# Softmax attention: ScalarE sums every fourth key tile's exponentials, three waves of ones per head instead of six

## The chip, the cores and the metric

One of the eight cores of a Trainium2 chip runs the whole program. Time is the device time of one execution in microseconds (us). The engines of a core work side by side, each through its own queue in order: TensorE (matrix products, PE in the views, with its weight loads as PEld), VectorE (DVE), ScalarE (ACT), GpSimd (POOL) and SyncE (SP, which issues most DMAs). They wait for each other through semaphores. SBUF is the working memory of 128 partitions; PSUM has eight banks of 128 x 512 numbers, into which TensorE writes.

## The reference

Four layers follow each other on `x` of shape (2, 2048, 512): a Mamba layer (L0), softmax attention (L1) and two linear attentions (L2, L3). The change lies in L1 alone:

```python
q = (xn @ q_w + q_b).reshape(Bx, Tx, H, -1)        # 16 heads of 32
k = (xn @ k_w + k_b).reshape(Bx, Tx, H, -1)
att = jnp.einsum('bnhl,bmhl->bnmh', q, k)
att = att + (1.0 - mask) * -1000000.0
att = jax.nn.softmax(att, axis=2)                  # over the keys
v = ((xn @ v_w + v_b) * src_mask[:, :, None]).reshape(Bx, Tx, H, -1)
y = jnp.einsum('bnmh,bmhl->bnhl', att, v)
```

With 2 batches and 16 heads there are 32 softmax problems of 2048 x 2048, called heads below. The softmax is the exact one: each query's maximum is taken off before the exponential.

## The kernel before, in words

`stage_attention` (from L1123) works through the 32 heads. It computes each head's scores twice.

*First pass, queries on partitions.* `max_mm` (L1263) makes one max tile: 128 queries (`qt`) against 512 keys (`kc`), in one of three PSUM banks `ps_max`. `reduce` (L1394) takes the maximum over the 512 keys on VectorE. 64 such tiles give a head's maxima `mx`; one small reduction (L1400) makes `m_all`, `turn_max` transposes it on TensorE, `first_part` (ScalarE, L1354) and `second_part` (VectorE, L1404) split it into two rows, and SyncE copies these into the stack of query rows by two DMAs (L1219). So the second pass gets its scores with the maximum already taken off.

*Second pass, keys on partitions.* `score_mm` (L1286) makes a tile of 128 keys (`kt`) against 512 queries, in one of three banks `ps_s`; `exp` (ScalarE, L1363) writes its exponentials into `prob`, which has four slots of 128 x 2048. `pv_mm` (L1296) multiplies a whole key tile's exponentials by the values into `ps_o`, which holds the sum over all 16 key tiles.

*Denominators.* GpSimd adds key tiles' exponentials element by element (L1251, in halves of 1024 columns) in groups of 2 or 3 tiles (`SIZES`, L1133), six groups a head. For each group `den_mm` (L1308) multiplies the sum by a matrix of ones and accumulates in `ps_d`: a wave of ones, four matmuls side by side in four column quarters of the array. `copy_o` and `copy_den` (ScalarE, L1369 and L1373) bring the output and the denominators to SBUF, `turn_o` transposes both, `read_o` (VectorE) takes the reciprocal (L1414) and writes the product to `v` (L1419).

*Order.* It is written out by hand. The main loop of TensorE goes over heads `hd` and units `u` (0 to 15), one key tile each. In unit `u` it issues, in turn, four score matmuls of key tile `u + 1` and four max matmuls that belong to the next head (from unit 13, `TURN_MAX`, to the one after that), then `pv_mm` of key tile `u`, and then what falls into this unit: a wave of ones (`DEN_LAG`, 2 units after a group's last key tile), `turn_o` of the head before (`TURN_O`, unit 2) or `turn_max` (unit 13). ScalarE does four exponentials per unit, then `copy_den` (unit 1), `first_part` (unit 13), and `copy_o` after unit 15. VectorE does four reductions per unit. A score matmul waits for the exponential three before it, a max matmul for the reader of the tile three before it (`free_bank`, L1258). Ahead of the first head, 64 max tiles of head 0 and 12 of head 1 are made with nothing else between them.

Of the kernel before, what the change touches and what calls it, by code (L numbers as in the profile page):

```python
# [1122 lines left out]
def stage_attention(nc, a, keep, parts, mask_parts, v):  # L1123

    with ExitStack() as ctx:
# [4 lines left out]
        NMAX = QT * QB  # L1130
        PER = NMAX // QT
        LEAD = 3
        SIZES = (2, 3, 3, 2, 3, 3)  # L1133
        GROUPS = [tuple(range(sum(SIZES[:g]), sum(SIZES[:g + 1]))) for g in range(len(SIZES))]
        NGRP = len(GROUPS)
        GROUP_END = {units[-1]: g for g, units in enumerate(GROUPS)}
        ADDS = sum(2 * (len(units) - 1) for units in GROUPS)
        used, sums = {}, {}
        for g, units in enumerate(GROUPS):
            for n, unit in enumerate(units[1:]):  # L1140
                for half in range(2):
# [4 lines left out]
        SLOTS = 4  # L1146
        HEADS = NB * H1
        TURN_MAX = QT - LEAD
        TURN_O = 2
        DEN_LAG = 2  # L1150
        q_st = [r.sb(f"q_stack{i}", [ROWS, S], F32R) for i in range(3)]
        k_st = [r.sb(f"k_stack{i}", [ROWS, S], F32R) for i in range(3)]
        prob = [r.sb(f"prob{i}", [P, S]) for i in range(SLOTS)]
# [12 lines left out]
        ps_o = r.ps("ps_o", [P, CH])  # L1166
        ps_d = r.ps("ps_d", [P, CH])
        names = ("ones_set rows_set max_in bank_filled bank_read m_done m_first m_second s_mm exp_done "
                 "o_mm o_copied sum_done den_mm den_copied den_turned den_inv den_read v_copied")
# [10 lines left out]
        def bank_items(hd):  # L1180
# [52 lines left out]
        @block.gpsimd  # L1233
        def _(pool):
            def take_v(hd):
                nc.gpsimd.tensor_copy(v_h[hd % 3][:, :, :], v[:, :, hd * DH1:(hd + 1) * DH1]).then_inc(s["v_copied"], 1)

            nc.gpsimd.memset(ones[:, :], 1.0).then_inc(s["ones_set"], 1)
            take_v(0)
            for hd in range(HEADS):  # L1240
                for g, units in enumerate(GROUPS):
                    if hd * NGRP + g >= 2:
                        pool.wait_ge(s["den_mm"], hd * NGRP + g - 1)
                    for n, unit in enumerate(units[1:]):
                        for half in range(2):
                            at = slice(half * HALF, (half + 1) * HALF)
                            pool.wait_ge(s["exp_done"], (hd * QT + unit) * QB + 2 * half + 2)
                            if n:
                                pool.wait_ge(s["sum_done"], hd * ADDS + used[units[n], half])
                            first = pair_sum[g % 2] if n else prob[units[0] % SLOTS]  # L1250
                            nc.gpsimd.tensor_tensor(pair_sum[g % 2][:, at], first[:, at], prob[unit % SLOTS][:, at],  # L1251
                                                    ALU.add).then_inc(s["sum_done"], 1)
                    if g == NGRP // 2 and hd + 1 < HEADS:
                        take_v(hd + 1)

        @block.tensor
        def _(pe):
            def free_bank(seq):  # L1258
                if seq >= BANKS:
                    pe.wait_ge(s["bank_read"], seq - BANKS + 1)  # L1260
                return ps_max[seq % BANKS]

            def max_mm(seq, hd, i):  # L1263
                slot = hd % 3
                if i == 0:
                    pe.wait_ge(stack_in[slot], (hd // 3 + 1) * NSTACK * 16)
                qt, kc = divmod(i, QB)
                nc.tensor.matmul(free_bank(seq)[:, :], q_st[slot][0:ROWS_MAX, qt * P:(qt + 1) * P],  # L1268
                                 k_st[slot][0:ROWS_MAX, kc * CH:(kc + 1) * CH], start=True, stop=True).then_inc(s["bank_filled"], 1)
# [38 lines left out]
            def den_mm(hd, g):  # L1308

                if g == 0 and hd:  # L1310
                    pe.wait_ge(s["den_read"], hd)
                pe.wait_ge(s["sum_done"], hd * ADDS + sums[g])
                for c in range(QB):
                    mm = nc.tensor.matmul(ps_d[c * DH1:(c + 1) * DH1, :], ones[:, :],
                                          pair_sum[g % 2][:, c * CH:(c + 1) * CH], start=(g == 0), stop=(g == NGRP - 1))
                mm.then_inc(s["den_mm"], 1)

            for i in range(NMAX):
# [29 lines left out]
        @block.scalar  # L1348
        def _(act):
            def first_part(seq, hd):  # L1350
                act.wait_ge(s["bank_filled"], seq + 1)
                if hd:
                    act.wait_ge(s["max_in"], hd * 32)
                nc.scalar.activation(m_parts[:, 0, :], ps_max[seq % BANKS][0:QT, 0:P], ACT.Copy, scale=-1.0).then_inc(s["m_first"], 1)  # L1354

            def exp(hd, kt, c):
                n = (hd * QT + kt) * QB + c
                act.wait_ge(s["s_mm"], n + 1)
                if hd * QT + kt >= SLOTS:
                    act.wait_ge(s["o_mm"], hd * QT + kt - SLOTS + 1)  # L1360
                    before, unit = divmod(hd * QT + kt - SLOTS, QT)
                    act.wait_ge(s["sum_done"], before * ADDS + used[unit, c // 2])
                nc.scalar.activation(prob[kt % SLOTS][:, c * CH:(c + 1) * CH], ps_s[n % BANKS][:, :], ACT.Exp).then_inc(s["exp_done"], 1)  # L1363

            def copy_o(hd):
                act.wait_ge(s["o_mm"], (hd + 1) * QT)
                if hd:
                    act.wait_ge(s["den_turned"], hd)
                nc.scalar.activation(o_raw[:, :], ps_o[:, :], ACT.Copy).then_inc(s["o_copied"], 1)  # L1369

            def copy_den(hd):
                act.wait_ge(s["den_mm"], (hd + 1) * NGRP)
                nc.scalar.activation(d_raw[:, :], ps_d[:, :], ACT.Copy).then_inc(s["den_copied"], 1)  # L1373

            first_part(NMAX, 0)
            for c in range(QB):
                exp(0, 0, c)
            for hd in range(HEADS):
                for u in range(QT):
                    for c in range(QB):  # L1380
                        if u + 1 < QT:
                            exp(hd, u + 1, c)
                        elif hd + 1 < HEADS:
                            exp(hd + 1, 0, c)
                    if u == TURN_O - 1 and hd:
                        copy_den(hd - 1)
                    if u == TURN_MAX and hd + 1 < HEADS:
                        first_part(item_at(hd, "turn_max", u), hd + 1)
                copy_o(hd)
            copy_den(HEADS - 1)  # L1390

        @block.vector
        def _(dve):
            def reduce(seq, hd, i):  # L1394
                qt, kc = divmod(i, QB)
# [579 lines left out]
```

## Time and profile before

| | us |
|---|---|
| median of 3 runs (lowest, highest) | 5740.84 (5740.23, 5743.70) |
| the profiled execution: its own time | 5742.74 |
| its span, first to last instruction | 5741.0 |
| mean granted TensorE clock | 0.973 |
| TensorE matmul busy | 5252.8 (91%) |
| VectorE busy | 4120.5 (72%) |
| GpSimd busy | 3280.1 (57%) |
| ScalarE busy | 2812.1 (49%) |

The rows further down come from one profiled execution. Starts are counted from its first instruction. In a row of the timeline, instructions of one line that follow each other are put together: `x4` with 2.06 us means that four of them lasted from the first start to the last end. In brackets stands how long the engine was idle before, and what ended that. The attention stage lies between about 2520 and 4351 us.

### The profile page before, as it was taken

To read this page: it belongs to the slowest core of one execution; us is meant where nothing else is said; L and a number is where in the kernel's file an instruction comes from. 1 tells how busy PE (TensorE), PEld (TensorE's weight loads), DVE (VectorE), ACT (ScalarE), POOL (GpSimd) and SP (SyncE) were. 2 spreads that over 40 slices of the span, in tenths; PEclk is the share of its full clock that TensorE was granted. 3 is DMA by queue.
4 is the path that set the end of the run, shared out by engine and by line. 5 is a ranking of instruction groups with operands and counts; after the bars stand their busy time and mean duration, and the time that the engine had idled before them with its cause. 6 is when DMAs were issued, how large, how long until landed. Compare 5 with 4: busy or idle time off the path is not lost. (4 is left out here: it accounts for less than half of the span.)

```text
span 5741.0 us, 58781 instructions
## 1 busy us (share of the span) xinstructions
PE 5252.8 (91%) x19584; PEld 2496.9 (43%) x19584; DVE 4120.5 (72%) x5430; ACT 2812.1 (49%) x4847; POOL 3280.1 (57%) x2136
## 2 busy tenths in 40 slices
PE   7888989888898869989999999999997899989998
PEld 2333333333333324445455455454543455454545
DVE  6999999999999972357777777777763455545454
ACT  4757566575757523326666666666662131312212
POOL 3879797887979751118888888888883000000000
PEclk9999999999999999979999999999999999999999
DMA  4021211212122114321111111111102301021101
GB/s 169 22 103 49 99 74 52 78 48 103 37 89 82 44 56 159 118 85 23 35 23 35 35 23 35 23 35 29 29 12 105 114 26 62 25 105 35 61 26 52
DMA packets 117503, 346.28 MB, mean 60 GB/s; under 512 B 13040, under 2 KB 14288, under 8 KB 102800
## 3 DMA queue, kind: packets, MB, share of 16 engines
q1 hardware_dynamic: 99280, 294.47, 15.7%
q0 software_dynamic: 9216, 33.56, 1.5%
q10 hardware_dynamic: 8704, 14.50, 0.7%
q8 instruction: 155, 2.54, 0.2%
q14 instruction: 148, 1.21, 0.1%
HBM read 274.29 MB, written 67.67 MB: 60 GB/s over the span
## 5 line engine op out<-in xcount | busy, mean ns | idle before, releaser
L1397 DVE TENSOR_REDUCE attn_mx<-attn_ps_max 128x1 f32<-128x512 f32 x2048 | 1269.5, 682 | 404.7 <-PE attn_ps_max L1268 400.1
L425 POOL TENSOR_TENSOR mamba_hc<-mamba_h,mamba_bc 128x1024 f32<-128x1024 f32 x512 | 1216.7, 2376 | 351.8 <-DVE mamba_h L658 298.0
L1363 ACT ACTIVATE attn_prob<-attn_ps_s 128x512 f32<-128x512 f32 x2048 | 1061.0, 604 | 589.8 <-PE attn_ps_s L1293 586.9
L805 PE MATMUL mamba_y<-mamba_hc,ident 128*128 128x512 f32 x2048 | 1008.2, 616 | 257.3 <-POOL mamba_hc L425 256.4
L1251 POOL TENSOR_TENSOR attn_pair_sum<-attn_prob 128x1024 f32<-128x1024 f32 x384 | 906.7, 2383 | 312.3 <-ACT attn_prob L1363 312.3
L528 ACT ACTIVATE mamba_da<-mamba_dt,mamba_a_neg 128x512 f32<-128x512 f32 x1024 | 689.5, 689 | 685.2 <-DVE mamba_h L658 682.1
L658 DVE TENSOR_TENSOR_SCAN mamba_h<-mamba_da,mamba_state,mamba_h 128x512 f32<-128x512 f32 x768 | 939.3, 1263 | 1.9 <-ACT mamba_da L528 1.9
L1293 PE MATMUL attn_ps_s<-attn_q_stack,attn_k_stack 100*128 100x512 f32 x2048 | 862.2, 424 | 4.2 <-ACT attn_prob L1363 4.2
L1268 PE MATMUL attn_ps_max<-attn_k_stack,attn_q_stack 98*128 98x512 f32 x2048 | 835.4, 415 | 16.5 <-DMA attn_q_stack<-qk_parts 16.0
L805 PEld LDWEIGHTS mamba_y<-mamba_hc,ident 128*128 128x128 f32 x2048 | 373.0, 193 | 838.4 <-POOL mamba_hc L425 421.3
L648 DVE TENSOR_TENSOR mamba_h<-mamba_du,mamba_bc 128x1024 f32<-128x1024 f32 x512 | 618.6, 1208 | 65.7 <-POOL mamba_state L427 57.5
L1251 POOL TENSOR_TENSOR attn_pair_sum<-attn_pair_sum,attn_prob 128x1024 f32<-128x1024 f32 x256 | 604.8, 2386 | 0.0
L1293 PEld LDWEIGHTS attn_ps_s<-attn_q_stack,attn_k_stack 100*128 100x128 f32 x2048 | 387.3, 190 | 455.5 <-ACT attn_prob L1363 232.2
L1304 PE MATMUL attn_ps_o<-attn_prob,attn_v_h 128*32 128x512 f32 x4096 | 546.4, 605 | 0.0
L1268 PEld LDWEIGHTS attn_ps_max<-attn_k_stack,attn_q_stack 98*128 98x128 f32 x2048 | 396.6, 194 | 133.4 <-DVE attn_mx L1397 40.3
L913 POOL TENSOR_TENSOR lin_norm_rstd<-lin_norm_var_eps,neg_half 128x4 f32<-128x4 f32 x16 | 16.1, 1007 | 606.8 <-DVE lin_norm_var_eps L902 606.8
L658 DVE TENSOR_TENSOR_SCAN mamba_h<-mamba_da,mamba_zeros,mamba_h 128x512 f32<-128x512 f32 x256 | 313.1, 1264 | 0.8 <-ACT mamba_da L528 0.8
L913 POOL TENSOR_TENSOR lin_out_norm_rstd<-lin_out_norm_var_eps,neg_half 128x4 f32<-128x4 f32 x16 | 16.1, 1006 | 515.6 <-DVE lin_out_norm_var_eps L902 515.6
L793 PE MATMUL mamba_work<-mamba_w,mamba_zy 128*128 128x512 f32 x512 | 253.9, 623 | 31.6 <-DVE mamba_x_in L676 31.1
L750 PE MATMUL mamba_work<-mamba_xn_t,mamba_w 128*128 128x512 f32 x512 | 249.4, 615 | 1.1 <-ACT mamba_xn_t L463 0.9
L761 PE MATMUL mamba_work<-mamba_xn_t,mamba_w 128*128 128x512 f32 x512 | 242.3, 595 | 0.0
L1651 PE MATMUL lin_mm_bank<-lin_w_q,lin_norm_xn_t 128*128 128x512 f32 x512 | 226.1, 595 | 8.4 <-DVE lin_q L1815 8.4
(232 smaller groups left out, 6077.6 us busy)
## 6 DMA issues: line engine op xcount, KB each, us to landing
mamba_bc<-bc_dram SPq DMA_DIRECT2D x64, 1024.0 KB, 7.3
mamba_w<-in_in_proj_w_T SPq DMA_DIRECT2D x16, 2048.0 KB, 7.8
qk_parts<-qkv_pair POOLq DMA_DIRECT2D x64, 512.0 KB
attn_k_stack<-qk_parts SPq DMA_DIRECT2D x96, 256.0 KB
attn_q_stack<-qk_parts SPq DMA_DIRECT2D x96, 256.0 KB
mamba_x_in<-in_x SPq DMA_DIRECT2D x16, 1024.0 KB, 5.3
mamba_w<-in_out_proj_w_T SPq DMA_DIRECT2D x8, 2048.0 KB, 8.6
lin_norm_x<-x_after_L SPq DMA_DIRECT2D x16, 1024.0 KB, 5.7
```

What stands on the lines that cost most here:

```text
L425: nc.gpsimd.tensor_tensor(hc[:, gs % HC_SLOTS, :, :], h[:, gs % H_SLOTS, :, :], bc[:, g, G:2 * G, :], ALU.mult).then_inc(s["hc_done"], 1)
L528: nc.scalar.activation(da[n % DA_BANKS][:, :], dt[:, ct % 2, :], ACT.Exp, scale=a_neg[:, ct, g * G + j:g * G + j + 1]).then_inc(s["exp_don ...
L648: nc.vector.tensor_tensor(h[:, gs % H_SLOTS, :, :], du[:, :].unsqueeze(1).to_broadcast([P, G, CH]), bc[:, g, 0:G, :], ALU.mult).then_inc(s ...
L658: nc.vector.tensor_tensor_scan(h[:, gs % H_SLOTS, j, :], da[(gs * G + j) % DA_BANKS][:, :], h[:, gs % H_SLOTS, j, :], first, ALU.mult, ALU ...
L793: mm = nc.tensor.matmul(at("out", it, t)[:, :], zy[:, k, t * P:(t + 1) * P], w_view("out", it)[:, k, :], start=(k == 0), stop=(k == CT - 1))
L805: mm = nc.tensor.matmul(y[ct % 2][:, :], ident[:, :], hc[:, gs % HC_SLOTS, j, :], start=(g == 0 and j == 0), stop=(g == NG - 1 and j == G ...
L1251: nc.gpsimd.tensor_tensor(pair_sum[g % 2][:, at], first[:, at], prob[unit % SLOTS][:, at], ALU.add).then_inc(s["sum_done"], 1)
L1268: nc.tensor.matmul(free_bank(seq)[:, :], q_st[slot][0:ROWS_MAX, qt * P:(qt + 1) * P], k_st[slot][0:ROWS_MAX, kc * CH:(kc + 1) * CH], start ...
L1293: nc.tensor.matmul(ps_s[n % BANKS][:, :], k_st[slot][0:ROWS, kt * P:(kt + 1) * P], q_st[slot][0:ROWS, c * CH:(c + 1) * CH], start=True, st ...
L1304: mm = nc.tensor.matmul(ps_o[c * DH1:(c + 1) * DH1, :], v_h[hd % 3][:, kt, :], prob[kt % SLOTS][:, c * CH:(c + 1) * CH], start=(kt == 0), ...
L1363: nc.scalar.activation(prob[kt % SLOTS][:, c * CH:(c + 1) * CH], ps_s[n % BANKS][:, :], ACT.Exp).then_inc(s["exp_done"], 1)
L1397: nc.vector.tensor_reduce(mx[hd % 3][:, qt, kc:kc + 1], ps_max[seq % BANKS][:, :], AX.X, ALU.max).then_inc(s["bank_read"], 1)
```

## The change

Key tiles 3, 7, 11 and 15 of a head are no longer added by GpSimd. Their part of each query's denominator comes from the first pass. The keys of a max tile are regrouped, so that block 3 of four holds just these four key tiles. For that block's tiles VectorE writes the negated maximum (`own_neg`), and ScalarE then makes one more activation on the same PSUM bank (`sum_own`): the exponential with `own_neg` as bias, whose sum over the row goes to `own_sum`. A max matmul that reuses the bank waits for that too. The sum stands against the block's own maximum, so it is scaled by exp(block maximum - head's maximum): GpSimd makes the difference (`make_gap`), ScalarE its exponential (`exp_gap`, after unit 5), GpSimd the product (`scale_own`), and VectorE adds it to the denominators ahead of the reciprocal. The other 12 key tiles form three groups of four. `TURN_O` goes from 2 to 3 and `DEN_LAG` from 2 to 3; the waves of ones then stand in units 7, 12, and 1 of the next head.

```diff
-        SIZES = (2, 3, 3, 2, 3, 3)
-        GROUPS = [tuple(range(sum(SIZES[:g]), sum(SIZES[:g + 1]))) for g in range(len(SIZES))]
-        NGRP = len(GROUPS)
+        OWN = QB - 1
+        SUMMED = [u for u in range(QT) if u % QB != OWN]
+        NGRP = 3
+        GROUPS = [tuple(SUMMED[g * len(SUMMED) // NGRP:(g + 1) * len(SUMMED) // NGRP]) for g in range(NGRP)]
...
-        TURN_O = 2
-        DEN_LAG = 2
+        TURN_O = 3
+        DEN_LAG = 3
+        GAP_AT = 5
...
+            def make_gap(hd):
+                pool.wait_ge(s["m_done"], hd + 1)
+                nc.gpsimd.tensor_tensor(own_gap[:, :], own_neg[hd % 3][:, :, 0], m_all[:, :], ALU.add).then_inc(s["gap_made"], 1)
+
+            def scale_own(hd):
+                pool.wait_ge(s["gap_exp"], hd + 1)
+                pool.wait_ge(s["own_summed"], (hd + 1) * QT)
+                if hd >= 2:
+                    pool.wait_ge(s["den_whole"], hd - 1)
+                nc.gpsimd.tensor_tensor(own_den[hd % 2][:, :], own_sum[hd % 3][:, :], own_gap[:, :], ALU.mult).then_inc(s["own_scaled"], 1)
...
             def free_bank(seq):
                 if seq >= BANKS:
                     pe.wait_ge(s["bank_read"], seq - BANKS + 1)
+                    if SEQ_OWN[seq - BANKS]:
+                        pe.wait_ge(s["own_summed"], OWN_BY[seq - BANKS + 1])
...
-                nc.tensor.matmul(free_bank(seq)[:, :], q_st[slot][0:ROWS_MAX, qt * P:(qt + 1) * P],
-                                 k_st[slot][0:ROWS_MAX, kc * CH:(kc + 1) * CH], start=True, stop=True).then_inc(s["bank_filled"], 1)
+                nc.tensor.matmul(free_bank(seq)[:, :].rearrange("p (a j) -> p a j", j=P), q_st[slot][0:ROWS_MAX, qt * P:(qt + 1) * P],
+                                 k_st[slot][0:ROWS_MAX, :].rearrange("r (a b j) -> r b a j", b=QB, j=P)[:, kc],
+                                 start=True, stop=True).then_inc(s["bank_filled"], 1)
...
+            def sum_own(seq, hd, i):
+
+                act.wait_ge(s["bank_read"], seq + 1)
+                nc.scalar.activation(own_exp[:, :], ps_max[seq % BANKS][:, :], ACT.Exp, bias=own_neg[hd % 3][:, i // QB, :],
+                                     accum_out=own_sum[hd % 3][:, i // QB:i // QB + 1]).then_inc(s["own_summed"], 1)
...
                             exp(hd + 1, 0, c)
+                    for j, tile in enumerate(max_tiles(hd, u)):
+                        if own_block(tile[1]):
+                            sum_own(item_at(hd, "max", u, j), *tile)
                     if u == TURN_O - 1 and hd:
                         copy_den(hd - 1)
                     if u == TURN_MAX and hd + 1 < HEADS:
                         first_part(item_at(hd, "turn_max", u), hd + 1)
+                    if u == GAP_AT:
+                        exp_gap(hd)
                 copy_o(hd)
...
+                to = own_neg[hd % 3][:, qt, :] if own_block(i) else mx[hd % 3][:, qt, kc:kc + 1]
+                nc.vector.tensor_reduce(to, ps_max[seq % BANKS][:, :], AX.X, ALU.max, negate=own_block(i)).then_inc(s["bank_read"], 1)
                 if i == NMAX - 1:
                     dve.wait_ge(s["bank_read"], seq + 1)
+                    nc.vector.tensor_reduce(mx[hd % 3][:, :, OWN:QB], own_neg[hd % 3][:, :, :], AX.X, ALU.max, negate=True
+                                            ).then_inc(s["m_own"], 1)
+                    dve.wait_ge(s["m_own"], hd + 1)
+                    if hd:
+                        dve.wait_ge(s["gap_made"], hd)
...
-                nc.vector.reciprocal(rden[:, :].rearrange("p (t c) -> p t c", c=QB),
-                                     ps_d[:, :].rearrange("p (t c e) -> p t c e", c=QB, e=DH1)[:, :, :, 0]).then_inc(s["den_inv"], 1)
+                dve.wait_ge(s["own_scaled"], hd + 1)
+                nc.vector.tensor_tensor(rden[:, :].rearrange("p (t c) -> p t c", c=QB),
+                                        ps_d[:, :].rearrange("p (t c e) -> p t c e", c=QB, e=DH1)[:, :, :, 0],
+                                        own_den[hd % 2][:, :].rearrange("p (c t) -> p t c", c=QB), ALU.add).then_inc(s["den_whole"], 1)
+                dve.wait_ge(s["den_whole"], hd + 1)
+                dve.sem_inc(s["den_read"], 1)
+                nc.vector.reciprocal(rden[:, :], rden[:, :]).then_inc(s["den_inv"], 1)
                 dve.wait_ge(s["den_inv"], hd + 1)
-                dve.sem_inc(s["den_read"], 1)
```

## Rows read from the trace of the kernel before

**Rows 1.** The page's costliest groups, GpSimd's first sums: x count, busy us, mean ns, idle before.
```profile
L1251 POOL TENSOR_TENSOR attn_pair_sum<-attn_prob 128x1024 f32<-128x1024 f32 x384 | 906.7, 2383 | 312.3 <-ACT attn_prob L1363 312.3
```

**Rows 2.** Stretches: us, busy us of each engine (instructions), granted clock, DMA share, GB/s.
```profile
2524.00:2580.00 56.00, 53.91 (x99) 26.48 (x100) 48.88 (x82) 4.82 (x10) 4.18 (x2) 0.50 0.24 54
2580.00:4295.00 1715.00, 1713.76 (x9654) 857.48 (x9656) 1262.60 (x2090) 1061.84 (x2071) 1468.71 (x649) 1.00 0.12 28
```

**Rows 3.** Line L1354, once a head from head 1: durations ns, first and last start.
```profile
L1354 ACT ACTIVATE attn_m_parts<-attn_ps_max x31: 266/266/268, 2623.2 to 4289.8; 16x128 fp32r<-16x128 f32 x31
```

**Rows 4.** Timeline of a plain unit: start us, us, engine, line.
```profile
3315.41 0.50 PE L1293 MATMUL attn_ps_s<-attn_q_stack,attn_k_stack 100*128 100x512 f32 x1
3315.95 2.06 ACT L1363 ACTIVATE attn_prob<-attn_ps_s 128x512 f32<-128x512 f32 x4 [1.02 <-PE attn_ps_s L1293]
3316.19 2.48 DVE L1397 TENSOR_REDUCE attn_mx<-attn_ps_max 128x1 f32<-128x512 f32 x4 [0.59 <-PE attn_ps_max L1268]
3316.93 0.40 PE L1293 MATMUL attn_ps_s<-attn_q_stack,attn_k_stack 100*128 100x512 f32 x1
3318.48 0.50 PE L1293 MATMUL attn_ps_s<-attn_q_stack,attn_k_stack 100*128 100x512 f32 x1
```

**Rows 5.** Timeline: first score matmuls of a unit with a wave, and of the next.
```profile
3279.95 0.50 PE L1293 MATMUL attn_ps_s<-attn_q_stack,attn_k_stack 100*128 100x512 f32 x1
3283.87 0.50 PE L1293 MATMUL attn_ps_s<-attn_q_stack,attn_k_stack 100*128 100x512 f32 x1
```

**Rows 6.** Timeline of ScalarE: activations with a bias, and a read of the accumulator.
```profile
68.94 0.69 ACT L513 ACTIVATE mamba_dt<-mamba_y,cols 128x512 f32<-128x512 f32 x1 [0.60 <-PE mamba_y L783]
69.53 0.68 ACT L514 ACTIVATE mamba_soft<-mamba_y,cols 128x512 f32<-128x512 f32 x1
...
4691.70 2.00 ACT L1743 ACTIVATE lin_k_t<-lin_k_t,lin_k_max 128x2048 f32<-128x2048 f32 x1 [14.73 <-DVE lin_k_max L1829]
4693.61 0.19 ACT L1743 ACTIVATION_READ_ACCUMULATOR lin_k_t<-lin_k_t,lin_k_max 128x1 f32 x1
4693.70 1.99 ACT L1743 ACTIVATE lin_k_t<-lin_k_t,lin_k_max 128x2048 f32<-128x2048 f32 x1
```

**Rows 7.** Timeline in the last head, where no max tiles are made.
```profile
4337.95 2.07 ACT L1363 ACTIVATE attn_prob<-attn_ps_s 128x512 f32<-128x512 f32 x4 [0.54 <-PE attn_ps_s L1293]
4338.60 0.19 PEld L1293 LDWEIGHTS attn_ps_s<-attn_q_stack,attn_k_stack 100*128 100x128 f32 x1 [0.66 <-ACT attn_prob L1363]
```

**Rows 8.** Timeline of ScalarE at a head's end.
```profile
3297.24 0.60 ACT L1369 ACTIVATE attn_o_raw<-attn_ps_o 128x512 f32<-128x512 f32 x1 [0.59 <-PE attn_ps_o L1304]
3297.74 1.08 ACT L1363 ACTIVATE attn_prob<-attn_ps_s 128x512 f32<-128x512 f32 x2
```

**Rows 9.** Timeline of VectorE after the output is turned.
```profile
3308.30 0.26 DVE L1414 RECIPROCAL attn_rden<-attn_ps_d 128x16 f32<-128x16 f32 x1 [0.94 <-PE attn_ps_d L1283]
3308.71 0.69 DVE L1419 TENSOR_TENSOR v<-attn_ps_max,attn_rden 128x512 f32<-128x512 f32 x1
```

**Rows 10.** Timeline after the maxima are turned; the rows' DMAs, line L1219.
```profile
3345.87 0.27 ACT L1354 ACTIVATE attn_m_parts<-attn_ps_max 16x128 fp32r<-16x128 f32 x1 [0.77 <-PE attn_ps_max L1273]
3346.17 0.28 DVE L1404 SCALAR_TENSOR_TENSOR attn_m_parts<-attn_ps_max,attn_m_parts 16x128 fp32r<-16x128 f32 x1 [0.42 <-ACT attn_m_parts L1354]
3349.62 0.19 PEld L1293 LDWEIGHTS attn_ps_s<-attn_q_stack,attn_k_stack 100*128 100x128 f32 x1 [0.84 <-DMA attn_q_stack<-attn_m_parts]
...
L1219 SPq DMA_DIRECT2D attn_q_stack<-attn_m_parts x64: 502/584/1126, 2565.4 to 4290.9; - x64
DMA to landing us min/median/max: 1.8/1.8/2.5
```

**Rows 11.** Timeline ahead of the first head.
```profile
2554.37 2.47 DVE L1397 TENSOR_REDUCE attn_mx<-attn_ps_max 128x1 f32<-128x512 f32 x4
2554.51 2.59 PE L1268 MATMUL attn_ps_max<-attn_k_stack,attn_q_stack 98*128 98x512 f32 x4
```

**Rows 12.** Timeline at the stage's end.
```profile
4346.58 0.20 PEld L1314 LDWEIGHTS attn_ps_d<-attn_pair_sum,attn_ones 128*32 128x32 f32 x8 [5.67 <-POOL attn_pair_sum L1251]
```

More of the change, by code:

```diff
@@ L1157, in stage_attention @@
         m_all = r.sb("m_all", [P, QT])
+        own_exp = r.sb("own_exp", [P, CH])
+        own_sum = [r.sb(f"own_sum{i}", [P, QT]) for i in range(3)]
+        own_neg = [r.sb(f"own_neg{i}", [P, QT, 1]) for i in range(3)]
+        own_gap = r.sb("own_gap", [P, QT])
+        own_den = [r.sb(f"own_den{i}", [P, QT]) for i in range(2)]
         m_parts = r.sb("m_parts", [QT, 2, P], F32R)
@@ L1168, in stage_attention @@
         names = ("ones_set rows_set max_in bank_filled bank_read m_done m_first m_second s_mm exp_done "
-                 "o_mm o_copied sum_done den_mm den_copied den_turned den_inv den_read v_copied")
+                 "o_mm o_copied sum_done den_mm den_copied den_turned den_inv den_read v_copied "
+                 "m_own gap_made gap_exp own_summed own_scaled den_whole")
         s = {n: r.sem(n) for n in names.split()}
@@ L1189, in bank_items, with own_block @@
             return items
+        def own_block(i):
+            return i % QB == OWN
         BEFORE = NMAX + 1 + LEAD * PER
@@ L1198, in item_at @@
             return first_item[hd] + bank_items(hd).index((kind, u, j))
+        SEQ_OWN = [own_block(i) for i in range(NMAX)] + [False] + [own_block(i) for i in range(LEAD * PER)]
+        for hd in range(HEADS):
+            SEQ_OWN += [kind == "max" and own_block(max_tiles(hd, u)[j][1]) for kind, u, j in bank_items(hd)]
+        OWN_BY = [0]
+        for own_here in SEQ_OWN:
+            OWN_BY.append(OWN_BY[-1] + own_here)
         @block.sync
@@ L1236, in take_v @@
                 nc.gpsimd.tensor_copy(v_h[hd % 3][:, :, :], v[:, :, hd * DH1:(hd + 1) * DH1]).then_inc(s["v_copied"], 1)
+            def make_gap(hd):
[7 more added lines that the diff above has]
+                nc.gpsimd.tensor_tensor(own_den[hd % 2][:, :], own_sum[hd % 3][:, :], own_gap[:, :], ALU.mult).then_inc(s["own_scaled"], 1)
             nc.gpsimd.memset(ones[:, :], 1.0).then_inc(s["ones_set"], 1)
             take_v(0)
+            make_gap(0)
             for hd in range(HEADS):
@@ L1249, in _ @@
                                 pool.wait_ge(s["sum_done"], hd * ADDS + used[units[n], half])
-                            first = pair_sum[g % 2] if n else prob[units[0] % SLOTS]
-                            nc.gpsimd.tensor_tensor(pair_sum[g % 2][:, at], first[:, at], prob[unit % SLOTS][:, at],
+                            first = pair_sum[(hd * NGRP + g) % 2] if n else prob[units[0] % SLOTS]
+                            nc.gpsimd.tensor_tensor(pair_sum[(hd * NGRP + g) % 2][:, at], first[:, at], prob[unit % SLOTS][:, at],
                                                     ALU.add).then_inc(s["sum_done"], 1)
@@ L1254, in _ @@
                         take_v(hd + 1)
+                    if g == 0:
+                        scale_own(hd)
+                if hd + 1 < HEADS:
+                    make_gap(hd + 1)
         @block.tensor
@@ L1314, in den_mm @@
                     mm = nc.tensor.matmul(ps_d[c * DH1:(c + 1) * DH1, :], ones[:, :],
-                                          pair_sum[g % 2][:, c * CH:(c + 1) * CH], start=(g == 0), stop=(g == NGRP - 1))
+                                          pair_sum[(hd * NGRP + g) % 2][:, c * CH:(c + 1) * CH], start=(g == 0), stop=(g == NGRP - 1))
                 mm.then_inc(s["den_mm"], 1)
@@ L1361, in exp @@
                     before, unit = divmod(hd * QT + kt - SLOTS, QT)
-                    act.wait_ge(s["sum_done"], before * ADDS + used[unit, c // 2])
+                    if (unit, c // 2) in used:
+                        act.wait_ge(s["sum_done"], before * ADDS + used[unit, c // 2])
                 nc.scalar.activation(prob[kt % SLOTS][:, c * CH:(c + 1) * CH], ps_s[n % BANKS][:, :], ACT.Exp).then_inc(s["exp_done"], 1)
@@ L1373, in copy_den, with exp_gap @@
                 nc.scalar.activation(d_raw[:, :], ps_d[:, :], ACT.Copy).then_inc(s["den_copied"], 1)
+            def sum_own(seq, hd, i):
+                act.wait_ge(s["bank_read"], seq + 1)
+                nc.scalar.activation(own_exp[:, :], ps_max[seq % BANKS][:, :], ACT.Exp, bias=own_neg[hd % 3][:, i // QB, :],
+                                     accum_out=own_sum[hd % 3][:, i // QB:i // QB + 1]).then_inc(s["own_summed"], 1)
+            def exp_gap(hd):
+                act.wait_ge(s["gap_made"], hd + 1)
+                nc.scalar.activation(own_gap[:, :], own_gap[:, :], ACT.Exp, scale=-1.0).then_inc(s["gap_exp"], 1)
+            for i in range(OWN, NMAX, QB):
+                sum_own(i, 0, i)
             first_part(NMAX, 0)
+            for i in range(OWN, LEAD * PER, QB):
+                sum_own(NMAX + 1 + i, 1, i)
             for c in range(QB):
@@ L1396, in reduce @@
                 dve.wait_ge(s["bank_filled"], seq + 1)
-                nc.vector.tensor_reduce(mx[hd % 3][:, qt, kc:kc + 1], ps_max[seq % BANKS][:, :], AX.X, ALU.max).then_inc(s["bank_read"], 1)
+                to = own_neg[hd % 3][:, qt, :] if own_block(i) else mx[hd % 3][:, qt, kc:kc + 1]
+                nc.vector.tensor_reduce(to, ps_max[seq % BANKS][:, :], AX.X, ALU.max, negate=own_block(i)).then_inc(s["bank_read"], 1)
                 if i == NMAX - 1:
                     dve.wait_ge(s["bank_read"], seq + 1)
+                    nc.vector.tensor_reduce(mx[hd % 3][:, :, OWN:QB], own_neg[hd % 3][:, :, :], AX.X, ALU.max, negate=True
[3 more added lines that the diff above has]
+                        dve.wait_ge(s["gap_made"], hd)
                     nc.vector.tensor_reduce(m_all[:, :], mx[hd % 3][:, :, :], AX.X, ALU.max).then_inc(s["m_done"], 1)
```

## The prediction

> **What bounds the kernel now.** I read the page first, then the totals by stretch, then single units of the attention stage on the timeline. The page's shares are means over four layers and can't tell: GpSimd's sums of exponentials, for one, are among its costliest groups [rows 1]. The stretches decide: from 2580 to 4295 us TensorE is busy for 1713.76 of 1715.00 us at the full clock, VectorE 1262.60, ScalarE 1061.84, GpSimd 1468.71 [rows 2]. One head takes (4289.8 - 2623.2) / 30 = 55.55 us [rows 3]. So TensorE's order is the bound, 31 times over; ScalarE has room on average. Whether it has room where the new work stands is the question, and an average can't tell.
>
> A plain unit (one key tile) shows it [rows 4]. Counted from its first score matmul at 3315.41, the next unit begins at +3.07 (I use 3.06, the spacing of most). The four exponentials start at +0.54, 0.48 apart (2.06 us for four of 0.60). The four reductions start at +0.78 and end at +3.26: the fourth reduction ends **after** the next unit has begun. The fourth score matmul starts at +1.52. A unit with a wave of ones takes 3283.87 - 3279.95 = 3.92, so a wave costs 0.86 [rows 5].
>
> **Waves of ones.** Six a head become three: 3 x 0.86 = 2.58 us a head off the path. Nothing lies beside it, TensorE does nothing else meanwhile. The same matrix work otherwise: the keys of a max tile are now read as four runs of 128 columns instead of one of 512. No row has such a read. The nearest are today's two kinds of matmul, which read different tiles at a spacing of 0.23 to 0.24: 0.01 either way on 64 tiles and 31 heads is 20 us either way. I take nothing, since most of each read stays contiguous, and keep both ends for the range.
>
> **The new exponential.** Each unit gets one 128x512 activation from PSUM with a per-partition bias, and a read of the accumulator. With such a bias two activations follow 0.57 to 0.59 apart (68.94 to 69.53) and last 0.68 [rows 6]. The read lasts 0.19, but starts 0.09 before its activation ends, and the next activation starts 0.09 after it [rows 6]. So the pair holds ScalarE for 0.58 + 0.09 = **0.67**. Bounds: 0.48, if it costs no more than today's exponentials; 0.88, if 0.69 and 0.19 stand end to end. I take 0.67, the nearest rows.
> The Trainium skill ("ScalarE: Activation LUTs", section "What ACT_TABLE_LOAD costs") gives an activation with a pointer bias 280 ns + 0.833 ns an element, with 93 ns of overlap. By it the activation is 0.71 and the pair 0.71 as an estimate; the rows read from PSUM say 0.68 and 0.67. By the page each head would come out some 0.3 us longer than in my sum.
>
> It stands behind the unit's four exponentials and waits for the fourth reduction: it starts at 3.26 + 0.03 = 3.29 and frees ScalarE at 3.95 in a unit of 3.06. Queued behind it are the next unit's exponentials, the first of which would start at 3.60. Who waits for these? Scores have three banks, so score matmul 4 waits for exponential 1 of the same unit. The last head, where no max tiles lie between, shows that wait today: the exponential ends at 4337.95 + 0.60 = 4338.55, the weight load follows at 4338.60 [rows 7], and a first matmul after a pause takes 0.50 instead of 0.40 [rows 4]: 0.05 + 0.10 = 0.15 from exponential to array; I use 0.14. Today that matmul starts at +1.52 and the exponential ended at 1.14, so 0.24 are spare.
>
> Now unit by unit, offsets from the unit's start, stalls at score matmul 4:
> - After a plain unit: first exponential 3.95 - 3.06 = 0.89, ends 1.49, matmul at 1.63 for 1.51: stall 0.12. The unit is 3.18 long, so the next one isn't late (0.77 + 0.60 + 0.14 = 1.51), and the stall comes in every second one: units 7, 9 and 11, 0.36 together.
> - After a unit with a wave (3.92): none.
> - Copy of the output at a head's end: it holds ScalarE 0.50 (3297.24 to 3297.74) [rows 8]. Before, it hid in the pause. Now the first exponential of unit 0 starts at 4.45 - 3.15 = 1.30, and 1.30 + 0.60 + 0.14 - 1.51 gives 0.52.
> - Copy of the denominators in unit 2: the same against 3.06, 0.62 in unit 3.
> - Turning the output (unit 3): 0.85 as before. What follows: today reciprocal at 3308.30, product at 3308.71 [rows 9], and the third max tile waits for its bank, 0.40. An addition stands ahead of the reciprocal now, 0.26 + 0.14 for the hand-over, less the 0.09 by which a reciprocal out of SBUF may be shorter: 0.70 in unit 4. Its reductions end late, so unit 5 loses 0.28.
> - Turning the maxima (unit 13, next head's rows): ScalarE's part waits behind the new activation, 3.95 - 3.09 = 0.86, +0.27, VectorE's part 0.28 [rows 10] ends at 1.44. The two rows land 2.42 after it (0.58 to the second issue, 1.84 to land; the view says 1.8). Today that lay under unit 14's wave (VectorE's part ends 3346.45, the score matmul comes at 3349.62) [rows 10]; the wave is gone from there and unit 14 lasts 1.44 + 2.42 + 0.05 = 3.91, a stall of 0.85. Unit 15 loses 0.09, unit 13 0.03.
> Sum of stalls: 0.36 + 0.52 + 0.62 + 0.85 + 0.70 + 0.28 + 0.85 + 0.12 = 4.30. Head: 16 x 3.06 + 3 x 0.86 + 4.30 = 55.84. The same sum for today: 48.96 + 5.16 + turns 0.84 + 0.40 + 0.13 = 55.49, against 55.55 in the trace. Difference **+0.35 a head**: the waves' 2.58 are spent on 2.9 of stalls. 31 x 0.35 = +10.9.
>
> **GpSimd, small steps.** GpSimd adds 18 halves a head for 20, 42.9 us at 2.385 [rows 1]; its two small products and the wait for the gap's exponential (0.2 us of ScalarE before a unit with slack) delay sums that nobody needs for several units: nothing. VectorE's extra small maximum, 0.3, falls into its 0.6 pause: nothing; uncovered it would be 10 us in all.
>
> **Once each.** Before the first head 64 + 12 max tiles run at VectorE's pace, 0.60, at the clock level 0.50 (1.2 GHz) [rows 2, 11]. A bank is refilled 0.06 after its read, the matmul takes 2.59 - 3 x 0.60 = 0.79. With the new activation: 0.03 + 0.67 + 0.09 + 0.06 + 0.79 + 0.03 = 1.67 from a reduction's end to the next in that bank, where 3 x 0.60 - 0.68 = 1.12 is today's (a reduction lasts 2.48 - 3 x 0.60 = 0.68). 17 tiles x 0.55 = +9.4. At the end TensorE waits 5.67 for GpSimd's sums [rows 12]; two sums less are -4.8, and about 1.1 of it, an estimate, goes to the pause before the last group of four, whose first sum needs two units later than today's: -3.7.
>
> Total 10.9 + 9.4 - 3.7 = +16.6 us. The profiled execution took 5742.74 (span 5741.0 and 1.7 around it), so it would take 5759.3. The median is 1.9 below it: **5757**.
>
> **Rivals.**
> 1. *ScalarE's room is enough* (not slower): score matmul 4 does not wait, because ScalarE gets past the new activation before it is needed. It decides at one point: the first exponential of a plain unit at or under +0.77. Then the three waves are all gained: -2.58 x 31 = -80, +9.4 - 3.7: 5667. For it: 1061.84 of 1715 busy. Against: the fourth reduction ends at 3.26 in any case, and both copies and both turns still stall by more than 0.4 each. Even at the lowest hold, 0.48, the sum gives only -0.8 a head. Chance 0.14, with what lies half way.
> 2. *The pair is a little cheaper or the restart shorter* (0.57 to 0.60 of hold): stalls in plain units vanish, -0.37 to -0.16 a head: 31 x -0.25 + 8 - 4 = -4, 5737. For it: 0.57 is the shortest spacing with a bias. Chance 0.26.
> 3. *The accumulator's read doesn't overlap* (0.88): each plain unit stalls, +1.8 a head, +13 ahead of the first head: 5741 + 56 + 13 - 4 = 5806. Against: its row shows the overlap. Chance 0.10.
>
> **Chances and range.** My forecast has 0.50, with its own range 5745 to 5772; most of it lies above +0.2% (11.5 us, about what a measurement tells from no change): 0.43 slower, 0.07 same. Rival 2: 0.22 same, 0.04 faster. Rival 1: 0.14 faster. Rival 3: 0.10 slower. Faster 0.18, same 0.29, slower 0.53. Range 5729 to 5790: it reaches to rival 2 and half way to rival 3.
>
> **What would show it.** In the changed trace: a spacing of heads of 55.9 (sum), 53 (rival 1), 57 (rival 3). ScalarE's new activation starting 3.29 into a unit, and its successor 0.67 later. Weight loads of scores waiting for ScalarE in units 0, 3 and 14; the score's first load of a head waiting for the DMA of the maxima's rows. Max tiles before the first head at 0.74 instead of 0.60. I am wrong if TensorE's wait for ScalarE is under 2 us a head, or if the clock level in 2580 to 4295 leaves 1.00.

## The result and the profile after

| | before | after |
|---|---|---|
| median of 5 runs beside each other (lowest, highest), us | 5740.84 (5739.8, 5744.1) | 5766.22 (5764.87, 5769.08) |
| ratio, 95% interval | | 1.0043 (1.0032 to 1.0055) |
| span of the profiled execution, us | 5741.0 | 5766.3 |

The changed kernel is slower by 25 us; the forecast was 16.6. First, from the page after, the costliest groups of the attention stage (the second answers to [rows 1], the third is the new activation), and from the lists of waits the one that grew, before and after (us in total, times, longest).

```profile
L1456 DVE TENSOR_REDUCE attn_mx<-attn_ps_max 128x1 f32<-128x512 f32 x1536 | 966.6, 683 | 375.8 <-PE attn_ps_max L1305 371.3
L1282 POOL TENSOR_TENSOR attn_pair_sum<-attn_prob 128x1024 f32<-128x1024 f32 x192 | 453.5, 2384 | 214.0 <-ACT attn_prob L1402 214.0
L1417 ACT ACTIVATE attn_own_exp<-attn_ps_max,attn_own_neg 128x512 f32<-128x512 f32 x512 | 352.3, 688 | 322.0 <-DVE attn_own_neg L1456 316.5
PEld attn_ps_s L1293 <- ACT attn_prob L1363: 232.2, 281, 0.8
PEld attn_ps_s L1331 <- ACT attn_prob L1402: 375.8, 626, 1.7
```

TensorE's wait for the exponentials grew by 143.6 us, 4.6 a head. The stretches (columns as in [rows 2]) and the once-a-head line (as in [rows 3]):

```profile
2524.00:2590.00 66.00, 49.38 (x87) 24.62 (x88) 50.30 (x82) 18.18 (x46) 0.42 (x2) 0.50 0.23 51
2590.00:4315.00 1725.00, 1683.68 (x8885) 803.28 (x8888) 1279.95 (x2152) 1397.63 (x3076) 1329.70 (x646) 1.00 0.12 28
L1392 ACT ACTIVATE attn_m_parts<-attn_ps_max x31: 249/249/267, 2635.8 to 4318.5; 16x128 fp32r<-16x128 f32 x31
```

TensorE had almost no gap before (1.2 us of 1715); now it is idle for 41 us of 1725, though three waves a head are gone, and ScalarE is busy for 81% of the stretch. A head takes (4318.5 - 2635.8) / 30 = 56.09 us for 55.55. The clock level is the same, 1.00.

Where the 25.3 us of span come from, by the first and last matmuls and products of both traces: 1.4 before the attention stage starts (the change touches nothing there; in the other runs below it is 0.05 to 2.4), 11.4 from the first max tile to the first score tile (58.1 for 46.8), 1.1 up to the first whole unit (no run takes this apart), 14.9 over 31 heads, -3.65 from the last head's start to its product, 0.1 after it.

Two plain units on the timeline, units 8 and 9 of head 10, as [rows 4]:

```profile
3178.54 0.68 DVE L1456 TENSOR_REDUCE attn_own_neg<-attn_ps_max 128x1 f32<-128x512 f32 x1
3179.03 0.50 PE L1331 MATMUL attn_ps_s<-attn_q_stack,attn_k_stack 100*128 100x512 f32 x1
3179.25 0.69 ACT L1417 ACTIVATE attn_own_exp<-attn_ps_max,attn_own_neg 128x512 f32<-128x512 f32 x1 [0.69 <-DVE attn_own_neg L1456]
3179.84 0.19 ACT L1417 ACTIVATION_READ_ACCUMULATOR attn_own_exp<-attn_ps_max,attn_own_neg 128x1 f32 x1
3179.93 2.05 ACT L1402 ACTIVATE attn_prob<-attn_ps_s 128x512 f32<-128x512 f32 x4
3180.57 0.19 PEld L1331 LDWEIGHTS attn_ps_s<-attn_q_stack,attn_k_stack 100*128 100x128 f32 x1 [0.24 <-ACT attn_prob L1402]
3182.23 0.50 PE L1331 MATMUL attn_ps_s<-attn_q_stack,attn_k_stack 100*128 100x512 f32 x1
```

The block's reduction ends at 3179.22, 0.19 after the next unit has begun. The new activation follows at once, holds ScalarE for 3179.93 - 3179.25 = 0.68, and the first exponential starts 0.90 into the unit (forecast 0.89, rival 1 needed 0.77) and ends at 3180.53 instead of 3180.17. Score matmul 4 waits for it, and the unit is 3.20 long. Just before the pair (the new activation and the read of its accumulator), ScalarE had stood idle for 0.69, waiting for that reduction.

All 16 units, medians over heads 2 to 28, worked out from the starts of the first score matmul of each unit:

```
unit      0    1    2    3    4    5    6    7    8    9    10   11   12   13   14   15
before   3.07 3.93 3.90 4.32 3.05 3.07 3.93 3.06 3.07 3.93 3.07 3.91 3.06 3.10 4.03 3.05
forecast 3.58 3.92 3.06 4.53 3.76 3.34 3.06 4.04 3.06 3.18 3.06 3.18 3.92 3.09 3.91 3.15
after    3.58 3.93 3.07 4.54 3.66 3.32 3.06 4.07 3.07 3.20 3.07 3.20 3.93 3.10 3.89 3.18
```

("Forecast" is the prediction's list added to its base of 3.06, the wave's 0.86 and the turn's 0.85.) Unit 14, where the maxima are turned and the rows' DMAs are due:

```profile
3196.41 0.25 ACT L1392 ACTIVATE attn_m_parts<-attn_ps_max 16x128 fp32r<-16x128 f32 x1
3196.69 0.28 DVE L1468 SCALAR_TENSOR_TENSOR attn_m_parts<-attn_ps_max,attn_m_parts 16x128 fp32r<-16x128 f32 x1 [0.99 <-ACT attn_m_parts L1392]
3199.43 0.19 PEld L1331 LDWEIGHTS attn_ps_s<-attn_q_stack,attn_k_stack 100*128 100x128 f32 x1 [0.99 <-DMA attn_q_stack<-attn_m_parts]
...
L1238 SPq DMA_DIRECT2D attn_q_stack<-attn_m_parts x64: 503/584/2004, 2576.9 to 4319.7; - x64
DMA to landing us min/median/max: 1.8/1.8/3.3
```

From the end of VectorE's part (3196.97) to the score's load are 2.46, in [rows 10] 3.17. In 9 of 30 heads the rows land 0.4 to 1.4 late, and the score's load follows 0.04 after they land in every head; the mean of unit 14 is 4.13 for its median of 3.89.

### The profile page after: what moved, and what is told of

Its sections match the earlier page's. It is cut to its first block and busy times, and to the rows that moved or that the text cites. A ratio compares the mean times of both kernels' runs of the same rounds, so it can differ in the third digit from the quotient of the medians.

```text
span 5766.3 us, 59004 instructions
## 1 busy us (share of the span) xinstructions
PE 5224.8 (91%) x18816; PEld 2443.0 (42%) x18816; DVE 4139.4 (72%) x5494; ACT 3168.2 (55%) x5903; POOL 3139.8 (54%) x2136
## 5 line engine op out<-in xcount | busy, mean ns | idle before, releaser
L1456 DVE TENSOR_REDUCE attn_mx<-attn_ps_max 128x1 f32<-128x512 f32 x1536 | 966.6, 683 | 375.8 <-PE attn_ps_max L1305 371.3
L1282 POOL TENSOR_TENSOR attn_pair_sum<-attn_pair_sum,attn_prob 128x1024 f32<-128x1024 f32 x384 | 904.3, 2386 | 37.9 <-ACT attn_prob L1402 37.9
L1331 PE MATMUL attn_ps_s<-attn_q_stack,attn_k_stack 100*128 100x512 f32 x2048 | 883.4, 434 | 34.6 <-ACT attn_prob L1402 24.1
L1282 POOL TENSOR_TENSOR attn_pair_sum<-attn_prob 128x1024 f32<-128x1024 f32 x192 | 453.5, 2384 | 214.0 <-ACT attn_prob L1402 214.0
L1417 ACT ACTIVATE attn_own_exp<-attn_ps_max,attn_own_neg 128x512 f32<-128x512 f32 x512 | 352.3, 688 | 322.0 <-DVE attn_own_neg L1456 316.5
L1456 DVE TENSOR_REDUCE attn_own_neg<-attn_ps_max 128x1 f32<-128x512 f32 x512 | 348.3, 680 | 6.6 <-PE attn_ps_max L1305 2.8
L750 PE MATMUL mamba_work<-mamba_xn_t,mamba_w 128*128 128x512 f32 x512 | 248.9, 614 | 1.1 <-ACT mamba_xn_t L463 0.9
```

Source lines behind the costliest of these rows:

```text
L1282: nc.gpsimd.tensor_tensor(pair_sum[(hd * NGRP + g) % 2][:, at], first[:, at], prob[unit % SLOTS][:, at], ALU.add).then_inc(s["sum_done"], 1)
L1331: nc.tensor.matmul(ps_s[n % BANKS][:, :], k_st[slot][0:ROWS, kt * P:(kt + 1) * P], q_st[slot][0:ROWS, c * CH:(c + 1) * CH], start=True, st ...
L1417: nc.scalar.activation(own_exp[:, :], ps_max[seq % BANKS][:, :], ACT.Exp, bias=own_neg[hd % 3][:, i // QB, :], accum_out=own_sum[hd % 3][: ...
L1456: nc.vector.tensor_reduce(to, ps_max[seq % BANKS][:, :], AX.X, ALU.max, negate=own_block(i)).then_inc(s["bank_read"], 1)
```

## The experiments

Each was timed beside the kernel before (median 5742.9 in both groups of runs); the ratios are the safer comparison with the changed kernel, whose 1.0043 gives 5767.6 beside 5742.9. "A head" is the spacing of the once-a-head line as above.

**small.** The new activation on one column.

```diff
-                nc.scalar.activation(own_exp[:, :], ps_max[seq % BANKS][:, :], ACT.Exp, bias=...
+                nc.scalar.activation(own_exp[:, 0:1], ps_max[seq % BANKS][:, 0:1], ACT.Exp, bias=...
```

> The changed kernel, with the new activation cut to one column of 512 (so the block's sum is left out but for one key; every wait stays). My theory: what costs is that the pair of activation and accumulator read holds ScalarE 0.67 us behind a reduction that ends at 3.26. With one column it holds 0.28, so plain units have no stall, unit 0 and unit 3 stall by 0.24 instead of 0.5 to 0.6, unit 14 by 0.47 instead of 0.85, unit 5 not at all; unit 4 keeps 0.70. Per head 54.3 instead of 56.1, 6.6 less ahead of the first head: 5700 to 5710 us (before: 5741). Rival, the wait for the reduction alone is what costs, not the work behind it: 5755 to 5766.

Measured: 5695.9, ratio 0.9919 (0.9906 to 0.9933), a head 54.10 for an expected 54.3, so 4 us below my range. Units 0 and 3 3.27 and 4.12, unit 14 3.47, unit 4 3.66, plain units 3.07. ScalarE's timeline in unit 9:

```profile
3150.66 0.26 ACT L1417 ACTIVATE attn_own_exp<-attn_ps_max,attn_own_neg 128x1 f32<-128x1 f32 x1 [0.69 <-DVE attn_own_neg L1456]
3150.82 0.19 ACT L1417 ACTIVATION_READ_ACCUMULATOR attn_own_exp<-attn_ps_max,attn_own_neg 128x1 f32 x1
3150.97 2.06 ACT L1402 ACTIVATE attn_prob<-attn_ps_s 128x512 f32<-128x512 f32 x4
```

The wait for the reduction stands as before, 0.69, and in plain units it costs nothing when the work behind it is short: the rival falls.

**third.** The same work, the block's tile third in the unit. Four of the seven changed lines:

```diff
+        OWN_AT = 2
+        BLOCKS = (0, 1, 3, 2)
...
-            return i % QB == OWN
+            return i % QB == OWN_AT
...
-                                 k_st[slot][0:ROWS_MAX, :].rearrange("r (a b j) -> r b a j", b=QB, j=P)[:, kc],
+                                 k_st[slot][0:ROWS_MAX, :].rearrange("r (a b j) -> r b a j", b=QB, j=P)[:, BLOCKS[kc]],
```

> The changed kernel with the summed block's max tile moved from fourth to third place in each unit; same work and same number of instructions. My theory: the third reduction ends at 2.66, so the new activation runs 2.69 to 3.36, in ScalarE's pause, and the next unit's first exponential (3.60) isn't late. Stalls left: unit 4 0.70, unit 14 0.27, the turn itself 0.85: about 53.6 a head, 5685 to 5697 us. Rival 1, ScalarE's total load is the limit (1398 of 1725 us): no change, 5766. Rival 2, the bank of the third tile is needed again sooner (second tile of the next unit, 3.86 against 3.59 when the sum is read) and max matmuls stall instead: 5730 or more.

Measured: 5690.7, ratio 0.9910 (0.9896 to 0.9923), a head 53.59, as expected. ScalarE's timeline (the unit's end is at 3151.54):

```profile
3151.17 0.69 ACT L1419 ACTIVATE attn_own_exp<-attn_ps_max,attn_own_neg 128x512 f32<-128x512 f32 x1
3151.76 0.19 ACT L1419 ACTIVATION_READ_ACCUMULATOR attn_own_exp<-attn_ps_max,attn_own_neg 128x1 f32 x1
3152.08 1.09 ACT L1404 ACTIVATE attn_prob<-attn_ps_s 128x512 f32<-128x512 f32 x2
```

The pair runs in the pause and the first exponential comes at 3152.08 - 3151.54 = 0.54, as before the change. ScalarE has the same work in less time (busy 1433.41 of 1655 us from 2590 to 4245), so its load isn't the limit; the place is. Unit 4 keeps 3.66, and max matmuls don't stall instead (plain units 3.07). This alone turns 25 us of loss into 52 of gain.

**wave14.** The second wave in unit 14 (`WAVE_AT = {7: 0, 14: 1}` for the rule with `DEN_LAG`).

> The changed kernel with the second wave of ones moved from unit 12 to unit 14, nothing else. My theory: unit 14 waits for the two rows of maxima (they land 2.42 after VectorE's part, in some heads up to 1.4 later), and a wave there covers 0.83 of it and most of the late landings: unit 12 goes from 3.93 to about 3.1, unit 14 stays at 3.9 in all heads. 5733 to 5743 us. Rival, the rows' landing isn't what unit 14 waits for (ScalarE's delay is): unit 14 grows by a wave, 5766.

Measured: 5758.25, ratio 1.0027 (1.0017 to 1.0037), a head 55.75: both expectations missed. Unit 12 lost its wave (3.07), unit 13 took the stall of every second unit (3.23), but unit 14 went to 4.47. On the timeline (the unit begins at 3191.52) three max matmuls wait for their banks one after the other: the first of these for the block's sum, which ends at 3192.34, the next for VectorE's part of the maxima, the last for a reduction that this part has put off. The wave comes behind that:

```profile
3192.15 0.19 ACT L1418 ACTIVATION_READ_ACCUMULATOR attn_own_exp<-attn_ps_max,attn_own_neg 128x1 f32 x1
3192.46 0.19 PEld L1306 LDWEIGHTS attn_ps_max<-attn_k_stack,attn_q_stack 98*128 98x128 f32 x1 [0.43 <-issue]
3192.91 0.19 PEld L1306 LDWEIGHTS attn_ps_max<-attn_k_stack,attn_q_stack 98*128 98x128 f32 x1 [0.16 <-DVEq L1473]
3193.69 0.19 PEld L1306 LDWEIGHTS attn_ps_max<-attn_k_stack,attn_q_stack 98*128 98x128 f32 x1 [0.47 <-DVE attn_mx L1457]
3195.01 1.04 PE L1353 MATMUL attn_ps_d<-attn_pair_sum,attn_ones 128*32 128x512 f32 x8
3195.98 0.19 PEld L1332 LDWEIGHTS attn_ps_s<-attn_q_stack,attn_k_stack 100*128 100x128 f32 x1 [0.84 <-DMA attn_q_stack<-attn_m_parts]
```

4.47 is 3.06 + 0.86 for the wave + 0.55 for these. The last row's 0.84 is named after the DMA, but the rows had landed 0.76 before it ended (2.41 after VectorE's part). The same 0.84 stands wherever a full-width load follows the narrow ones of 32 columns (median of 353 places where a score's load follows the products with the values in the changed kernel), so it belongs to the narrow matmuls ahead of the load and not to the DMA, also in [rows 10]. In unit 14 of the changed kernel the two waits overlap: the banks' wait (0.68 there, by the start of the products with the values) lies inside the 0.83 by which the rows lengthen the unit. A wave placed behind the first covers the second and adds itself to the first. (My expectation placed ScalarE's lateness in this unit at score matmul 4; it shows at the banks.) What it did cover are most late landings: heads 1 to 29 are all between 55.68 and 55.95.

**noadd.** No addition ahead of the reciprocal (the block's share is left out of the denominators).

> The changed kernel without VectorE's addition ahead of the reciprocal (the block's share of the denominator is left out; its waits and GpSimd's steps stay). My theory: unit 4 gets 0.25 to 0.3 shorter, all else the same: 5756 to 5759 us. Rival, the chain after the turned output isn't on the path once ScalarE is late in unit 5 anyway: 5766.

Measured: 5761.7, ratio 1.0034 (1.0022 to 1.0046); unit 4 3.56 for 3.66, a gain of 0.10 where 0.25 to 0.3 was expected, so the range was missed by 3 us. VectorE's timeline of the changed kernel, then of this one:

```profile
3162.12 0.17 DVE L1479 TENSOR_TENSOR attn_rden<-attn_ps_d,attn_own_den 128x16 f32<-128x16 f32 x1 [1.33 <-PE attn_ps_d L1321]
3162.44 0.25 DVE L1484 RECIPROCAL attn_rden<-attn_rden 128x16 f32<-128x16 f32 x1
3162.73 0.69 DVE L1487 TENSOR_TENSOR v<-attn_ps_max,attn_rden 128x512 f32<-128x512 f32 x1
```

```profile
3160.95 0.26 DVE L1479 RECIPROCAL attn_rden<-attn_ps_d 128x16 f32<-128x16 f32 x1 [1.33 <-PE attn_ps_d L1321]
3161.46 0.69 DVE L1485 TENSOR_TENSOR v<-attn_ps_max,attn_rden 128x512 f32<-128x512 f32 x1 [0.25 <-PE attn_ps_max L1305]
```

From its first start to the product the chain is 0.61 for 0.41 in [rows 9], 0.20 more. My edit put both semaphore steps (`sem_inc`) between the reciprocal and the product, and the chain is 0.51. From the end of one instruction to the start of the next it is 0.04 with no such step between them, 0.15 with one and 0.25 with two (no run changes this number alone). The chain got 0.10 shorter and unit 4 too, so it is on the path and the rival falls.

**prolog.** One column only ahead of the first head.

> The changed kernel, with the new activation cut to one column only for the tiles made ahead of the first head (head 0 and the lead of head 1; their block sums are left out but for one key). My theory: ahead of the first head each fourth tile costs 3.05 - 2.40 = 0.65 more because its bank is refilled only after the sum is read; with one column the pair holds 0.28 and the bank comes 0.39 sooner: 17 x 0.39 = 6.6 us less, heads unchanged: 5759 to 5761 us (changed kernel 5766). Rival, VectorE's pace still sets that stretch: no change.

Measured: 5759.0, ratio 1.0028 (1.0017 to 1.0038), 7 less than the changed kernel by the medians, 9 by the ratios, at the edge of the range; a head 56.07, unchanged. The first score tile comes 50.9 after the first max tile, for 58.1 and 46.8: of the 11.4 added there, 7.2 hang on the pair's length. The changed kernel's timeline there:

```profile
2556.32 0.68 DVE L1456 TENSOR_REDUCE attn_own_neg<-attn_ps_max 128x1 f32<-128x512 f32 x1
2557.04 0.69 ACT L1417 ACTIVATE attn_own_exp<-attn_ps_max,attn_own_neg 128x512 f32<-128x512 f32 x1 [2.27 <-DVE attn_own_neg L1456]
2557.62 0.19 ACT L1417 ACTIVATION_READ_ACCUMULATOR attn_own_exp<-attn_ps_max,attn_own_neg 128x1 f32 x1
2557.93 0.92 PEld L1305 LDWEIGHTS attn_ps_max<-attn_k_stack,attn_q_stack 98*128 98x128 f32 x3 [1.18 <-DVE attn_mx L1456]
2559.37 0.68 DVE L1456 TENSOR_REDUCE attn_own_neg<-attn_ps_max 128x1 f32<-128x512 f32 x1
```

Four tiles take 3.05 instead of 2.40: 17 x 0.65 = 11.

**six.** The added part alone: `SIZES`, `TURN_O` and `DEN_LAG` as before the change, with the new activations and the scaling (block 3 counts twice in the denominators).

> One part of the change alone: the new activations, their waits and the scaling as in the changed kernel, but all 16 key tiles summed by GpSimd and six waves of ones as before (units 1, 3, 6, 9, 11, 14; the denominators count block 3 twice). My theory: the added work costs, by the same sum, 0.5 in unit 0, 0.6 in unit 3, 0.1 in units 5, 8, 11 and 13, 0.5 in unit 14: about 57.1 a head, 5790 to 5802 us with the stretch ahead of the first head. Rival, the waves left more room on ScalarE, and the pair costs only where waves are missing: 5755 to 5765.

Measured: 5816.85, ratio 1.0129 (1.0115 to 1.0142), a head 57.55, 15 above my range's upper end. Against the kernel before, unit 6 has a stall too (4.03 for 3.93), which I had left out; unit 0 grew by 0.63 instead of 0.5, and units 5, 8, 11 and 13 by 0.13 to 0.15 instead of 0.1. The two parts of the change are thus: added work +74 us; waves and GpSimd's fourth tiles taken away (with `TURN_O` and `DEN_LAG` 3 for 2) -49 (1.0043 x 5742.9 = 5767.6, less 5816.85), not the -84 of 31 x 2.58 and the tail's 3.7. The rest is what the waves had covered: unit 4 is 3.66 in the changed kernel and 3.07 here, and unit 14 gets only 0.58 shorter by the medians (3.89 for 4.47) and 0.39 by the means when its wave of 0.86 goes.

**third_turns.** "third", with the turns ahead of the products with the values, and ScalarE's `first_part` ahead of `sum_own`:

```diff
+                    if u == TURN_O and hd:
+                        turn_o(item_at(hd, "turn_o", u), hd - 1)
+                    if u == TURN_MAX and hd + 1 < HEADS:
+                        turn_max(item_at(hd, "turn_max", u), hd + 1)
                     pv_mm(hd, u)
```

> The kernel 'third' with both turns (output in unit 3, maxima in unit 13) put ahead of the products with the values instead of behind them, and ScalarE's part of the maxima ahead of the new activation. My theory: VectorE's chain after a turn then lies under 1.1 us of TensorE's own work: unit 4 goes from 3.66 to 3.07, unit 14 from 3.33 to 3.07 in most heads; each turn costs some 0.15 because it waits for the reader of its bank. Per head 52.9 instead of 53.6: 5665 to 5674 us. Rival, the chain starts as late as before because it waits for the fourth reduction, or the turn's wait for its bank gives the gain back: 5685 to 5691.

Measured: 5679.7, ratio 0.9891 (0.9877 to 0.9904), a head 53.30. Unit 4 is 3.07 and unit 14 3.07, as expected; but units 3 and 13 cost 0.27 and 0.30 instead of 0.15, and the time is 6 us above my range. TensorE's loads idle 0.44 to 0.47 before the turn, and it begins 0.11 after the second reduction of the unit, which reads the turn's bank. Unit 14's mean is 3.24: the rows still land late in some heads.

**best.** "third_turns" and "wave14" together.

> The kernel 'third_turns' with the second wave of ones moved to unit 14 as well. My theory: in 'wave14' the wave didn't pay in full because ScalarE's lateness (0.55 at score matmul 4) stood ahead of it in the same unit; here ScalarE isn't late, so the wave covers late landings of the maxima's rows at no cost: unit 14 at 3.93 in every head, unit 12 at 3.07, 0.1 to 0.2 a head less than 'third_turns': 5660 to 5670 us. Rival, late landings were already covered there: same time as 'third_turns'.

Measured: 5671.9, ratio 0.9878 (0.9863 to 0.9894), a head 53.12; 29 of 31 heads lie between 53.06 and 53.19. That is 2 us above my range. The 0.18 a head gained on "third_turns" is what its late rows cost (3.24 - 3.07 in unit 14's mean); unit 14 is now 3.92 in the median and 3.93 in the mean, so the rival falls. Its stretches and its once-a-head line:

```profile
2590.00:4230.00 1640.00, 1636.16 (x8915) 835.62 (x8907) 1273.98 (x2152) 1425.86 (x3086) 1337.08 (x650) 1.00 0.13 29
L1395 ACT ACTIVATE attn_m_parts<-attn_ps_max x31: 249/266/267, 2631.4 to 4225.0; 16x128 fp32r<-16x128 f32 x31
```

It beats both kernels, by 71 us (beside each other) and by 94 us (medians). ScalarE is busier (1425.86 of 1640) than in the changed kernel.

## Why the prediction was right, and where its sizes were off

- *The bound and the place of the new work.* Right: ScalarE's pair costs by standing behind a reduction that ends after its unit. "small" (shorter), "third" (earlier) and the units' table show it; 15 of 16 units are within 0.03 of the list in their medians.
- *The total.* 25.3 of span for 16.6: the heads took 14.9 for 10.9, the stretch ahead of the first head 11.4 for 9.4, and 1.1 + 1.4 more stand outside the sum. The nearness owes something to luck: within the heads one term was 3 us too large and a missing one 7.4 us.
- *The pair's hold,* 0.67: measured 0.68. The estimate of 0.71 by the Trainium skill ("ScalarE: Activation LUTs", section "What ACT_TABLE_LOAD costs") was too long: the rows of another line of this kernel were nearer.
- *Four runs of 128 columns,* nothing: the max matmul's median is 397 ns for 395, and plain units without a stall kept 3.07.
- *Turning the output,* +0.31 in unit 4: measured 0.20 in the chain. Within the term, the addition lasts 0.17, not 0.26, its hand-over 0.15 for 0.14, and the reciprocal out of SBUF is not shorter by 0.09 (0.25 for 0.26). And the hand-over from the reciprocal to the product shrank from 0.15 to 0.04, because the semaphore step moved ahead of the reciprocal. Unit 4 is 3.66, not 3.76: 3 us too much.
- *The rows' landing,* 2.42: right in two heads of three. The sum had no term for late ones. In [rows 10] they lay under a wave (3 of 30 were late there). 31 x (4.13 - 3.89) = **7.4 us**, the largest miss. The profiled executions of the other changed kernels have 7 to 12 heads of 31 whose rows land over 0.3 late, so it isn't an accident of one trace.
- *Ahead of the first head,* +9.4: measured 11.4. The load comes at 2557.93, 0.12 after the sum is read (2557.81), not 0.06; it waits for two semaphores there, the reduction's and the sum's, but no run tells whether that is why.
- *The tail,* -3.7: -3.65 up to the last product. GpSimd's last sum ends 47.1 after the last head's first score matmul for 51.0 before, so its sums set the end as the term had it; TensorE's wait for them fell only from 5.67 to 4.30, since its own part of the head is shorter too.
- *Rival 1* (room enough, 5667) fell here, but names what the order gives away: "best" is 5672 with the same added work. Rivals 2 and 3 had the hold wrong (0.57 to 0.60 and 0.88 for 0.68).

Still open: why some rows land late, and in more heads than before; no run changed these DMAs.

## What to carry to other kernels

Ask of added work not whether its engine has room on average, but what it waits for and what stands behind it in the queue: moved one place forward in its unit, the same activation turned a loss of 25 us into a gain of 52. Move the producer it waits for earlier in the unit before counting on the pause. And when a wave or other cover is removed, look up what it covered; when one is put back, look at what stands ahead of it in the same unit, since waits overlap and work adds.

## What was not expected of the hardware

- Two small DMAs of 8 KB each land 1.8 us after their issue in most heads, but up to 3.3 in the changed kernel, with the DMA engines busy for 12% of the stretch.
- A weight load that waits for two semaphores came 0.12 us after the later event (2557.81 to 2557.93), one with a single wait 0.05 after [rows 7].
